# A graph network's edge loop: VectorE's product of one-hots and weights in one instruction per chunk or in four

## What is computed

```python
# layer 0: a spline convolution; 8 kernels of 64x64, and 8 weights for each edge
weights, idx = _spline_basis(edge_attr_3)              # [E, 8], products of the 3 attributes or 1 - them
z   = (B[:, :, None] * x[src][:, None, :])             # each edge: 8 weighted copies of the source's row
agg = segment_sum(z.reshape(E, 8 * 64) @ W.reshape(512, 64), dst)
out = agg / max(count(dst), 1) + x @ root
x   = layernorm(x + elu(batchnorm(out)))
# layer 1
agg = segment_sum(x[src] + edge_attr_64, dst)
x   = layernorm(x + batchnorm(relu(agg @ W1 + b1) @ W2 + b2))
```

## Time and profile before

| what | us |
|---|---|
| median of 3 runs | 596.18 |
| lowest and highest of them | 589.14 and 597.19 |
| the profiled execution's own time | 601.57 |
| its span, first to last instruction | 599.8 |
| busy: TensorE, its weight loads | 508.7, 407.9 |
| busy: VectorE, ScalarE, GpSimd | 407.5, 367.9, 375.2 |

### The profile page before, as it was taken

How to read it: one execution, slowest core, us unless ns; L and a number is a source line. 1 busy time by engine, 2 the same in 40 slices (tenths; PEclk the granted TensorE clock), 3 DMA queues, 4 the chain that set the end, 5 groups by cost and what they waited for, 6 DMA issues and landing times.

```text
span 599.8 us, 13973 instructions
## 1 busy us (share of the span) xinstructions
PE 508.7 (85%) x4151; PEld 407.9 (68%) x4151; DVE 407.5 (68%) x1624; ACT 367.9 (61%) x662; POOL 375.2 (63%) x382
## 2 busy tenths in 40 slices
PE   4269998997797998896997898797997998799993
PEld 2258877876686877685886777686886887344532
DVE  6996885875755676575675666476476554879875
ACT  7575995885867786685785777674242232450054
POOL 6777777777777777777777777777777760000000
PEclk9998997998989998898898989799575556699997
DMA  7633553544535344345343445352244110000002
GB/s 144 140 87 74 120 117 78 124 111 109 126 78 118 89 109 111 89 106 118 72 118 100 104 108 119 71 119 64 45 96 75 25 25 3 0 1 1 1 2 53
DMA packets 89144, 48.75 MB, mean 81 GB/s; under 512 B 76252, under 2 KB 77667, under 8 KB 89069
## 3 DMA queue, kind: packets, MB, share of 16 engines
q1 hardware_dynamic: 75949, 35.40, 24.9%
q0 software_dynamic: 11968, 12.28, 10.9%
q10 hardware_dynamic: 1152, 0.16, 0.2%
HBM read 46.86 MB, written 0.93 MB: 80 GB/s over the span
## 4 chain that ended last, share of the span: by engine, by line
PE 50%; POOL 19%; DMA 11%; DVE 8%; issue 8%; ACT 2%; DVEq 0%; SPq 0%; POOLq 0%; ACTq 0%
POOL rows L529 19%; PE ps L681 11%; DMA rows<-in_x,idx 10%; PE ps L640 9%; PE ps L600 8%; PE ps L860 6%; PE ps L625 5%; PE ps L865 2%; PE ps L619 2%; DVE pair L1298 1%; PE ps L608 1%; PE ps L715 1%; PE ps L893 1%; PE ps L589 1%; PE ps L630 1%
## 5 line engine op out<-in xcount | busy, mean ns | idle before, releaser
L529 POOL DMA_INDIRECT rows<-in_x,idx x374 | 373.9, 1000 | 116.2 <-issue 101.8
L681 PE MATMUL ps<-whot_room,rows 128*128 128x96 f32 x816 | 183.3, 311 | 44.8 <-DMA rows<-in_x,idx 43.0
L681 PEld LDWEIGHTS ps<-whot_room,rows 128*128 128x128 f32 x816 | 145.1, 220 | 57.2 <-issue 37.1
L1001 ACT CAST adj<-ps 125x500 f32 x208 | 122.9, 591 | 89.3 <-PE ps L608 76.3
L988 ACT ACTIVATE u<-u,own 128x768 uint8<-128x768 uint8 (+1 forms) x168 | 152.5, 958 | 28.5 <-DMA u<-codes_scratch 28.5
L600 PE MATMUL ps<-pair,ohp 128*125 128x300 bf16 (+1 forms) x416 | 151.3, 366 | 14.4 <-DVE ohp L1302 8.9
L1298 DVE TENSOR_SCALAR pair<-iota_h,comb 128x300 bf16<-128x300 int16 (+1 forms) x416 | 104.1, 313 | 62.0 <-PE ps L608 60.3
L640 PE MATMUL ps<-xs,u 125*128 125x192 bf16 x1050 | 138.1, 258 | 2.6 <-issue 1.5
L1302 DVE TENSOR_SCALAR ohp<-iota_h,srcp 128x125 bf16<-128x125 int16 x416 | 108.4, 273 | 1.3 <-issue 1.3
L640 PEld LDWEIGHTS ps<-xs,u 125*128 125x128 fp8e4 x1050 | 96.1, 106 | 13.0 <-issue 3.5
L1313 DVE TENSOR_TENSOR agg<-agg,ps 128x24 f32 x416 | 75.6, 182 | 35.7 <-PE ps L625 29.9
(11 more groups left out here) (209 smaller groups left out, 381.6 us busy)
## 6 DMA issues: line engine op xcount, KB each, us to landing
u<-codes_scratch SPq DMA_DIRECT2D x42, 400.0 KB, 4.2
rows<-in_edge_attr SPq DMA_DIRECT2D x51, 256.0 KB
rows<-in_x,idx POOLq DMA_INDIRECT x374
x_now<-in_x SPq DMA_DIRECT2D x25, 31.2 KB
adj<-in_x SPq DMA_DIRECT2D x1, 700.0 KB
xs<-in_x SPq DMA_DIRECT2D x1, 700.0 KB
out<-u SPq DMA_DIRECT2D x3, 224.0 KB
adj<-in_edge_attr SPq DMA_DIRECT2D x1, 576.0 KB
```

What stands on the lines that cost most here:

```text
L529: pool.indirect_dma_start(rows[:, s, t, 0:C], None, x, bass.IndirectOffsetOnAxis(ap=idx[:, at:at + 1], axis=0)).then_inc(gathered[0][0] if ...
L681: last = nc.tensor.matmul(z_ps[:, half, at:at + ZW], rows[:, s, t, :], whot[:, par, t, :], start=True, stop=True)
L1001: nc.scalar.copy(bass.AP(adj, offset=start, ap=[[NT * NA, PN], [NA, NT], [1, GWIN]]), m_ps[0:PN, bank_of(phase, g), 0:PAIRS].rearrange("p ...
```

## The change

The one product of `build_weights` becomes four, each over two tiles (`STEP` is 2): 192 elements in a partition in place of 768. All four write the same `whot` and read the same `hot` and `basis` as before; the two waits stand ahead of the first, and the last one sets `whot_ready`. Nothing else is changed.

```diff
             def build_weights(c, par):
                 dve.wait_ge(whot_used, c)
                 dve.wait_ge(hot_ready, c + 1)
-                nc.vector.tensor_tensor(
-                    whot[:, par, :, :].rearrange("p t (k w) -> p t k w", k=KIN),
-                    hot[:, :, :].rearrange("p t (a w) -> p t a w", a=1).to_broadcast([P, CH, KIN, WIN]),
-                    basis[:, bass.ds(c * CH, CH), :].rearrange("p t (k a) -> p t k a", a=1
-                                                               ).to_broadcast([P, CH, KIN, WIN]),
-                    ALU.mult).then_inc(whot_ready, 1)
+                for t in range(0, CH, STEP):
+                    last = nc.vector.tensor_tensor(
+                        whot[:, par, t:t + STEP, :].rearrange("p t (k w) -> p t k w", k=KIN),
+                        hot[:, t:t + STEP, :].rearrange("p t (a w) -> p t a w", a=1).to_broadcast([P, STEP, KIN, WIN]),
+                        basis[:, bass.ds(c * CH + t, STEP), :].rearrange("p t (k a) -> p t k a", a=1
+                                                                         ).to_broadcast([P, STEP, KIN, WIN]),
+                        ALU.mult)
+                last.then_inc(whot_ready, 1)
```

## The result

The changed kernel takes 590.82 us (median of 20 runs, 586.47 to 597.58) against 596.12 (20 runs, 589.14 to 601.07): a ratio of 0.9921 with a 95% interval of 0.9897 to 0.9945. That is 5.3 us less by the medians, within the 2% that was called no change, and clear of zero. The profiled execution took 587.40 us, 14.2 less than that of before; it lies near the low end of its runs, and that of before (601.57) above the high end of its own, so the two traces show the mechanism well and the size too large.

What follows compares the result with a forecast made beforehand. The prediction took GpSimd's gathers, held by VectorE's product, as the loop's pace. Holds of 14.3 less 4.0 save 10.3 us, less 1.0 off the path is 9.3; 596.18 - 9.3 = 586.9 us, range 579 to 594.

Steps and rivals of the forecast that it cites:

- TensorE keeps part of it: Rival, last seven chunks: TensorE at the lower clock throughout loses some 4 us of the gain, 591 us; chance 0.14.
- GpSimd is the pace of the loop: Edge loop, line 529: GpSimd turns out gathers end to end, 0.30 us before each, never truly waiting for anybody.
- The product shuts a gather out from 0.14 us after its start to its end: Line 1289 against line 529: one product shuts GpSimd out for 0.81 us; 43 gathers took 14.3 us over the median.
- The rival by which nothing is held: Rival, lines 529 and 1289: the product isn't what holds a gather, nothing is saved, 596 us; chance 0.05.
- Four products: 355 ns each, 1.18 us together: VectorE, line 1289: four small products take 1.18 us instead of 0.955 per chunk, 11.7 us more in 52 chunks.
- Covered, as said: VectorE's added 11.7 us cost nothing: it waits for TensorE some 2.5 us per chunk, and weights are two chunks ahead.
- A gather gets in between two products; 4.0 us of holds are left: Line 529: 0.06 us stay open between two small products, so holds cost 0.074 us per chunk, about 4.0 in all.
- The proof that the prediction gave for it: The gather at 31.81 went on at 32.61, though VectorE's next instruction, line 1342, had started at 32.52.
- The rival of the whole burst: Rival, line 529: a waiting gather doesn't get in between the four products; about 8 us more, 604; chance 0.05.
- GpSimd saves 14.3 - 4.0 = 10.3 us: Gathers, line 529: holds by products fall from 14.3 to about 4.0 us, saving 10.3 us by the last gather.
- On the path 9.3, next late is TensorE; gathers behind 449 us don't matter: Loop's end: TensorE runs gap-free after its last wait, so 1.0 of the 10.3 us is lost, leaving 9.3.
- TensorE gap-free at the lower clock from before 420: Sign of being wrong, at the loop's end; the prediction expected TensorE's last wait for rows near 445 instead.

Runs made afterwards that it cites:

- warm: Changed kernel plus twelve matmuls nobody reads in each of the seven chunks whose follower has no products of line 640: 586.94 us, ratio 0.9838.
- the two kernels whose end follows GpSimd: Kernel before and changed kernel, each with twelve unread matmuls added in each of seven late chunks: 594.40 and 586.94 us.

## Why the prediction was right, and where its size was off

The time lies in the stated range, and the change acts by the mechanism that was forecast. But of the 9.3 us forecast 5.3 came, and 590.82 is the time that the prediction gave to its rival *TensorE keeps part of it*, 591, and not to its forecast, 586.9.

- *GpSimd is the pace of the loop.* Right. Its gaps stayed at 0.3 us in every run. The last gather came 11.0 us later with the product done twice and 4.2 with eight products, and the medians of the timed runs rose by 12.6 and 5.4; the ends of the loop in the same profiles moved by 7.0 and 0.4, since the tail behind the last gather differs from execution to execution.
- *The product shuts a gather out from 0.14 us after its start to its end.* Right, for pieces of 768, 384 and 192 elements. The rival by which nothing is held falls: 43 gathers meet the product, and those that are held go on within 0.01 us of its end. The note on tensor_tensor in the Trainium skill, "SBUF — State Buffer", section "Who interferes with whom", isn't borne out here for indirect DMAs that take their row numbers from SBUF, while its rule on two SBUF inputs against a GpSimd read agrees with these traces. That it is the reading of the row numbers that is held, no run shows.
- *Four products: 355 ns each, 1.18 us together.* 352 and 1.15, the group 60.5 us as forecast. Covered, as said: in none of the three profiles of the changed kernel (one of them warm) does TensorE wait for `whot` in the loop. The reason given was too wide, though. The 2.5 us of VectorE's waits in a chunk are an average and no reserve that each chunk has: with 0.87 us more, in the product done twice, TensorE waited for `whot` six times.
- *A gather gets in between two products; 4.0 us of holds are left.* 4.8, 4.5 and 4.4 in three profiles. A single gather wasn't let in: in each of the three, one near 37 or 38 us, some 0.68 us behind the first start, was held 0.48 us, to the fourth's end. The proof that the prediction gave for it, the gather at 31.81, is one case: ahead of the same instruction a gather was not let in with eight products. The rival of the whole burst, which was drawn against four products, is in the main what happens with eight.
- *GpSimd saves 14.3 - 4.0 = 10.3 us.* This term was mis-sized. 14.3 us came from one profiled execution, and the holds of a whole product are 8.9 to 14.7 in five; that the timed runs lie at the low side is read from the two kernels whose end follows GpSimd, which differ by 7.5 us.
- *On the path 9.3, next late is TensorE; gathers behind 449 us don't matter.* The other mis-sized term. TensorE's last wait for rows wasn't near 445 but at 462.28, and what follows it depends on the clock of the last seven chunks, which differs between executions of one kernel (7.5 and 10.0 us from the last gather to the loop's end). The prediction named TensorE gap-free at the lower clock from before 420 as a sign of being wrong, and the second profile shows just that, from 419 to 480 (the first from 418 to 452, 33.86 busy of 34.00). Warming shows the price: 2.2 us before, 3.9 after. The rival that gave TensorE 4 us of the gain, 591, had that mechanism, but the net of it is 3.9 - 2.2 = 1.7. Together 7.5 - 1.7 = 5.8, which shares out the difference of these medians (596.65 - 590.82) and is no check on it; beside its own runs of before the change measured 5.3.

## What to carry to other kernels

An engine with a modest busy share can be the pace: look whether its idle time is the same small gap ahead of each instruction, and whether single instructions are longer than their median, and set the other engine's row beside those. A sum read from such meetings in one profile is one draw; a second profile, or a version in which nothing else can bind the end, gives its spread. And where an engine of the path saves, ask what clock the follower has in the stretch where the saving arrives.

## What the runs showed of the hardware that was not expected

Eight products of 96 elements, started 0.17 us apart, shut GpSimd's gathers out to the end of the eighth once four of them had passed, and five gathers beyond it; four products of 192, started 0.27 apart, let them in after each but for one or two gathers in each profile, and eight with a memset between, started 0.22 apart, let them in too. Why the fifth differs from the first three isn't settled. TensorE was granted the lower of its two clock levels, 0.50, through 61 us in which it was busy for 60.95 (changed kernel, second profile); with twelve more matmuls in each of the last chunks it was granted 0.95 from 445 to 482 us.
